# Block 4's query and key rows in spread order, and a recurrence whose decays run four groups ahead

## The reference

```python
# block 3, x: 800 rows of 256; W_aiv: 256 x 3072
a_proj, i_proj, v = jnp.split(x @ W_aiv, 3, axis=-1)
a = sigmoid(a_proj + decay_bias);  i = sigmoid(i_proj)
input_signal = jnp.sqrt(jnp.maximum(1.0 - a * a, 1e-08)) * (i * v)
h = _chunked_scan(a, input_signal)      # chunks of 64; logs clipped at 1e-10
return h @ W_mix + b_mix
# block 4, 16 heads, DK = 16
q, k, v = query @ Wq.T + bq, key @ Wk.T + bk, value @ Wv.T + bv
scores = where(mask, einsum('bhtd,bhsd->bhts', q, k) / sqrt(DK), -inf)
return softmax(scores) @ v @ Wo.T + bo
```

## Time and profile before

| | us |
|---|---|
| median of 3 runs | 506.22 |
| lowest, highest | 499.56, 510.32 |
| the profiled execution | 508.15 |
| its span | 506.4 |
| the recurrence, first projection to last of `h @ W_mix` | 233.44 to 330.54 |
| block 4's first maximum | 352.18 |
| block 4's last output projection ends | about 492 |

### The profile page before, as it was taken

One profiled execution on the slowest core, in us unless ns is written; L12 is line 12 of the kernel. 1 busy time (PEld: TensorE's weight loads), 2 busy tenths in 40 slices (PEclk: granted clock), 3 DMA queues, 4 the chain that ended last, 5 costly groups with the idle time before them and its releaser, 6 DMA issues.

```text
span 506.4 us, 7332 instructions
## 1 busy us (share of the span) xinstructions
PE 429.4 (85%) x2920; PEld 280.8 (55%) x2920; DVE 265.5 (52%) x481; ACT 163.3 (32%) x334; POOL 130.1 (26%) x174
## 2 busy tenths in 40 slices
PE   2999986959999974997999999961979969979986
PEld 1556743535667754874555557640346646646654
DVE  5056676992146520236675998651953634643423
ACT  0440430004531231322537424021143534523731
POOL 4620075327441066056100000006003213300100
PEclk9999998969999886999999999995575795975989
DMA  8991020001116963320000029976175256320002
GB/s 242 363 246 37 1 63 27 0 0 45 44 45 192 370 262 113 84 71 20 1 2 0 0 37 134 126 128 90 37 111 75 38 71 91 62 31 2 3 1 65
DMA packets 30616, 42.17 MB, mean 83 GB/s; under 512 B 4330, under 2 KB 27286, under 8 KB 30186
## 3 DMA queue, kind: packets, MB, share of 16 engines
q1 hardware_dynamic: 28279, 35.95, 28.6%
q0 software_dynamic: 2304, 5.76, 7.1%
HBM read 33.00 MB, written 8.98 MB: 83 GB/s over the span
## 4 chain that ended last, share of the span: by engine, by line
PE 65%; DVE 11%; DMA 10%; POOL 6%; ACT 4%; issue 3%; SPq 1%; ACTq 0%; DVEq 0%; POOLq 0%
PE banks L1193 13%; PE banks L1259 6%; PE banks L951 5%; PE banks L1299 5%; PE banks L1286 5%; DMA RC<-NT 4%; PE banks L1006 4%; PE banks L980 3%; PE banks L1227 3%; PE banks L940 2%; DVE RA L449 2%; PE banks L1031 2%; PE banks L1112 2%; PE banks L1130 2%; DMA RC<-q_parts 2%
## 5 line engine op out<-in xcount | busy, mean ns | idle before, releaser
L1604 DVE TENSOR_REDUCE NM<-banks 100x2 f32<-100x722 f32 x64 | 57.2, 906 | 63.2 <-PE banks L1259 62.4
L1193 PE MATMUL banks<-XT,RBG 128*128 128x400 f32 x192 | 65.0, 500 | 2.1 <-ACT XT L744 2.1
L1193 PEld LDWEIGHTS banks<-XT,RBG 128*128 128x128 f32 x192 | 36.3, 190 | 29.8 <-issue 1.2
L899 ACT ACTIVATE CT<-banks 128x400 f32<-128x400 f32 (+1 forms) x72 | 35.9, 504 | 41.9 <-PE banks L1286 40.8
L598 POOL TENSOR_TENSOR rstd<-ve,mhalf 100x4 f32<-100x4 f32 x12 | 12.5, 1040 | 140.0 <-DVE ve L1359 140.0
L744 ACT ACTIVATE XT<-banks 128x800 f32<-128x800 f32 x14 | 11.6, 838 | 98.6 <-PE banks L940 98.6
L1259 PE MATMUL banks<-RBG,RC 97*100 97x361 bf16 x64 | 23.1, 464 | 13.6 <-DMA RC<-q_parts 12.2
L940 PE MATMUL banks<-identf,XN 100*128 100x100 f32 x112 | 17.1, 309 | 17.5 <-DVE XN L1364 10.0
L1299 PE MATMUL banks<-CT,RV 128*17 128x100 f32 (+1 forms) x576 | 28.4, 293 | 0.0
L1286 PE MATMUL banks<-RC,RBG 100*128 100x100 bf16 (+1 forms) x192 | 21.7, 254 | 7.6 <-DMA RC<-NT 7.6
L1286 PEld LDWEIGHTS banks<-RC,RBG 100*128 100x128 bf16 (+1 forms) x192 | 18.3, 140 | 15.4 <-DMA RC<-NT 8.7
(11 more groups left out here) (228 smaller groups left out, 832.8 us busy)
## 6 DMA issues: line engine op xcount, KB each, us to landing
RA<-in_L_ffn_W SPq DMA_DIRECT2D x2, 2048.0 KB, 11.8
k_parts<-RA SPq DMA_DIRECT2D x18, 180.5 KB, 3.4
RBG<-in_L_attn_W_aiv SPq DMA_DIRECT2D x1, 3072.0 KB, 16.1
CT<-in_ctx_t SPq DMA_DIRECT2D x2, 1444.0 KB, 11.4
RC<-q_parts SPq DMA_DIRECT2D x12, 200.0 KB, 6.7
RBG<-k_parts SPq DMA_DIRECT2D x12, 180.5 KB, 8.8
RA<-k_parts SPq DMA_DIRECT2D x12, 180.5 KB, 9.1
RBG<-k_parts POOLq DMA_DIRECT2D x12, 180.5 KB, 6.5
```

Source lines behind the costliest of these rows:

```text
L899: sc.activation(P4[slot][0:n, g * HG * T:(g + 1) * HG * T], PS[4 + w % 2][0:n, 0:HG * T], ACT.Exp).then_inc(st_exp, 1)
L1193: ins = mm(PS[2 * aiv_pair(i) + g][:, 0:GC], WA[:, k, c:c + P], XT[:, k, GC * g:GC * g + GC], start=(k == 0), stop=(k == KT - 1))
L1604: v.tensor_reduce(NM[:, b % 2, 2 * i:2 * i + 2], PP[w % 2][0:T, :, 0:S], AX.X, ALU.max, negate=True).then_inc(mx_out, 1)
```

## The change

In the recurrence TensorE projects a0 to a3 first, then i and v of a group and the a of the group four further on. The order is a list, `AIV`, and all waits are looked up in it. The running decay is scanned into `UU[:, j]`, which is not yet in use, and capped there in an instruction of its own; the square root, floored, is multiplied with it into `SQ[j]` (`weight`), from a alone. Only then ScalarE may write the sigmoid of i into `UU[:, j]` (`weights_done`). `SQ` has eight slots. i times v, that times the weight, and the scan of the states follow (`states`). POOL writes the zero column of `UU` group by group, and block 5's weights are made behind the fourth group's states. In block 4, row r of a part's product d is now `6 * d + r` instead of `16 * r + d`, for queries and keys alike: each transfer still writes 16 partitions, every sixth one.

```diff
+AHEAD = 4
-        SQ = [part(CTF, 808 * i, B, TP) for i in range(4)]
-        CD = part(CTF, 808 * 4, B, TP)
+        SQ = [part(CTF, 808 * i, B, TP) for i in range(7)] + [part(RA, 6464, B, TP)]
-                    queue.dma_start(QS[DK * r:DK * r + DK, g].rearrange("d (k h) n -> d k (h n)", h=HK),
+                    queue.dma_start(QS[r:ROW_MASK:len(PARTS), g].rearrange("d (k h) n -> d k (h n)", h=HK),
-                queue.dma_start(KS[s][DK * r:DK * r + DK].rearrange("d (k h) s -> d k (h s)", h=HK),
+                queue.dma_start(KS[s][r:ROW_MASK:len(PARTS)].rearrange("d (k h) s -> d k (h s)", h=HK),
+        AIV = [(0, j) for j in range(AHEAD)] + [
+            x for j in range(RT) for x in [(1, j), (2, j)] + [(0, j + AHEAD)] * (j + AHEAD < RT)]
...
+            def sigmoids(w, j):
+                act.wait_ge(aiv_mm, AIV.index((w, j)) + 1)
+                if w == 1:
+                    act.wait_ge(weights_done, j + 1)
...
+            for j in range(AHEAD):
+                sigmoids(0, j)
+                if j >= 1:
+                    squares_of(j - 1)
+            squares_of(AHEAD - 1)
+            roots_of(range(AHEAD))
+            for j in range(AHEAD):
+                sigmoids(1, j)
+                sigmoids(0, j + AHEAD)
+                if j >= 1:
+                    squares_of(j + AHEAD - 1)
+            squares_of(RT - 1)
+            roots_of(range(AHEAD, RT))
+            for j in range(AHEAD, RT):
+                sigmoids(1, j)
...
+            def decays(j):
+                bt, cd = BT[j % 2], UU[:, j]
...
+                v.tensor_tensor_scan(flat(cd), flat(DEC[:, j]), flat(bt), 0.0, ALU.mult, ALU.max
+                                     ).then_inc(cdec, 1)
+                dve.wait_ge(cdec, j + 1)
+                v.tensor_scalar(flat(cd), flat(cd), 1.0, None, ALU.min).then_inc(capped, 1)
+            def weight(j):
+                dve.wait_ge(roots, j + 1)
...
+                v.scalar_tensor_tensor(out=flat(SQ[j]), in0=flat(SQ[j]), scalar=1e-4, in1=flat(UU[:, j]),
+                                       op0=ALU.max, op1=ALU.mult).then_inc(weights_done, 1)
+            def states(j):
...
+                v.tensor_tensor(o, o, src, ALU.mult).then_inc(iv_done, 1)
...
+                v.tensor_tensor(flat(UU[:, j]), flat(SQ[j]), flat(UU[:, j]), ALU.mult).then_inc(u_done, 1)
...
+            clamp(0)
+            for j in range(AHEAD):
+                if j + 1 < AHEAD:
+                    clamp(j + 1)
+                decays(j)
+            for j in range(AHEAD):
+                weight(j)
+            for j in range(AHEAD):
+                states(j)
+                clamp(j + AHEAD)
+                decays(j + AHEAD)
...
+            for j in range(AHEAD, RT):
+                weight(j)
+            for j in range(AHEAD, RT):
+                states(j)
```

More of the change, by code:

```diff
@@ L189, in build @@
         CTF = CT[:].rearrange("p k s -> p (k s)")
-        SQ = [part(CTF, 808 * i, B, TP) for i in range(4)]
-        CD = part(CTF, 808 * 4, B, TP)
-        BT = [part(CTF, 808 * (5 + i), B, TP) for i in range(2)]
+        SQ = [part(CTF, 808 * i, B, TP) for i in range(7)] + [part(RA, 6464, B, TP)]
+        BT = [part(SELT[:].rearrange("p a b -> p (a b)"), 808 * i, B, TP) for i in range(2)]
         V4 = part(RV, 0, B * NJ, H, VW)
@@ L315, in build @@
         clamped = sem("clamped")
+        capped = sem("capped")
+        weights_done = sem("weights_done")
+        u_pads = sem("u_pads")
         iv_done = sem("iv_done")
@@ L438, in k_buffer, with aiv_pair @@
             return b % 2 if b < 6 else b - 4
-        def aiv_pair(i):
-            return (i + 2) % 4
+        AIV = [(0, j) for j in range(AHEAD)] + [
+            x for j in range(RT) for x in [(1, j), (2, j)] + [(0, j + AHEAD)] * (j + AHEAD < RT)]
+        SIGS = [x for x in AIV if x[0] < 2]
+        def aiv_pair(w, j):
+            return (AIV.index((w, j)) + 2) % 4
         def y_before(L):
@@ L703, in _ @@
             gp.memset(DEC[:, :, :, 0:1], 0.0)
-            gp.memset(UU[:, :, :, 0:1], 0.0)
             for t in BT:
@@ L709, in _ @@
             bias(3)
+            for j in range(RT):
+                pool.wait_ge(weights_done, j + 1)
+                gp.memset(UU[:, j, :, 0:1], 0.0).then_inc(u_pads, 1)
             rsqrt(4)
@@ L853, in _ @@
             act.wait_ge(pads, 1)
[L854 to L865, removed]
-                act.wait_ge(clamped, j + 1)
[L867 to L875, removed]
@@ new lines, in sigmoids @@
+            def sigmoids(w, j):
+                act.wait_ge(aiv_mm, AIV.index((w, j)) + 1)
+                if w == 1:
+                    act.wait_ge(weights_done, j + 1)
+                for g in range(G):
+                    src = PS[2 * aiv_pair(w, j) + g][:, 0:GC].rearrange("p (b t) -> p b t", b=GB)
+                    if w == 0:
+                        ins = sc.activation(DEC[:, j, GB * g:GB * g + GB, 1:TP], src, ACT.Sigmoid,
+                                            bias=CB[:, C_DEC + j:C_DEC + j + 1])
+                    else:
+                        ins = sc.activation(UU[:, j, GB * g:GB * g + GB, 1:TP], src, ACT.Sigmoid)
+                ins.then_inc(sig, 1)
@@ new lines, in squares_of, with roots_of @@
+            def squares_of(j):
+                act.wait_ge(clamped, j + 1)
+                sc.activation(SQ[j], DEC[:, j], ACT.Square).then_inc(squares, 1)
+            def roots_of(js):
+                for j in js:
+                    act.wait_ge(squares, j + 1)
+                    sc.activation(SQ[j], SQ[j], ACT.Sqrt, scale=-1.0, bias=onesf[:, 0:1]).then_inc(roots, 1)
+            for j in range(AHEAD):
+                sigmoids(0, j)
+                if j >= 1:
+                    squares_of(j - 1)
@@ L1189, in aiv @@
             def aiv(i, g):
-                j, w = i // 3, i % 3
+                w, j = AIV[i]
                 for k in range(KT):
                     c = w * REC + j * P
-                    ins = mm(PS[2 * aiv_pair(i) + g][:, 0:GC], WA[:, k, c:c + P], XT[:, k, GC * g:GC * g + GC],
-                             start=(k == 0), stop=(k == KT - 1))
+                    ins = mm(PS[2 * aiv_pair(w, j) + g][:, 0:GC], WA[:, k, c:c + P],
+                             XT[:, k, GC * g:GC * g + GC], start=(k == 0), stop=(k == KT - 1))
                 return ins
@@ L1206, in _ @@
                 if i >= 4:
-                    jp, wp = (i - 4) // 3, (i - 4) % 3
+                    wp, jp = AIV[i - 4]
                     if wp < 2:
-                        pe.wait_ge(sig, 2 * jp + wp + 1)
+                        pe.wait_ge(sig, SIGS.index((wp, jp)) + 1)
                     else:
@@ L1542, in flat, with clamp @@
                 return t.rearrange("p b t -> p (b t)")
-            def inputs(j):
-                dve.wait_ge(roots, j + 1)
-                v.scalar_tensor_tensor(out=flat(UU[:, j]), in0=flat(SQ[j % 4]), scalar=1e-4, in1=flat(UU[:, j]),
-                                       op0=ALU.max, op1=ALU.mult).then_inc(u_done, 1)
+            def clamp(j):
+                a_t = DEC[:, j, :, 1:TP]
+                dve.wait_ge(sig, SIGS.index((0, j)) + 1)
+                v.tensor_scalar(a_t, a_t, FLOOR, 1.0, ALU.max, ALU.min).then_inc(clamped, 1)
+            def decays(j):
+                bt, cd = BT[j % 2], UU[:, j]
+                dve.wait_ge(clamped, j + 1)
+                v.tensor_scalar(bt[:, :, 1 + CHUNK:2 + CHUNK], DEC[:, j, :, 1 + CHUNK:2 + CHUNK],
+                                1.0 / FLOOR, None, ALU.mult).then_inc(reset64, 1)
+                dve.wait_ge(reset64, j + 1)
+                v.tensor_tensor_scan(flat(cd), flat(DEC[:, j]), flat(bt), 0.0, ALU.mult, ALU.max
[3 more added lines that the diff above has]
+            def weight(j):
+                dve.wait_ge(roots, j + 1)
+                dve.wait_ge(capped, j + 1)
+                v.scalar_tensor_tensor(out=flat(SQ[j]), in0=flat(SQ[j]), scalar=1e-4, in1=flat(UU[:, j]),
+                                       op0=ALU.max, op1=ALU.mult).then_inc(weights_done, 1)
+            def states(j):
+                dve.wait_ge(sig, SIGS.index((1, j)) + 1)
+                dve.wait_ge(aiv_mm, AIV.index((2, j)) + 1)
+                o = UU[:, j, :, 1:TP].rearrange("p (g b) t -> p g b t", g=G)
+                src = PP[aiv_pair(2, j)][:, :, 0:GC].rearrange("p g (b t) -> p g b t", b=GB)
+                v.tensor_tensor(o, o, src, ALU.mult).then_inc(iv_done, 1)
+                dve.wait_ge(iv_done, j + 1)
+                dve.wait_ge(u_pads, j + 1)
+                v.tensor_tensor(flat(UU[:, j]), flat(SQ[j]), flat(UU[:, j]), ALU.mult).then_inc(u_done, 1)
                 dve.wait_ge(u_done, j + 1)
@@ L1553, in _ @@
             dve.wait_ge(pads, 1)
[L1554 to L1585, removed]
@@ L1586, in _ @@
-            for j in range(RT - 4, RT):
-                inputs(j)
+            clamp(0)
[9 more added lines that the diff above has]
+                decays(j + AHEAD)
```

(11 more changed lines are left out.)

## The result

| | before | after |
|---|---|---|
| median, us | 506.63 (499.56 to 510.32, 4 runs) | 478.18 (477.83 to 479.65, 4 runs) |
| profiled execution, us | 508.15 | 479.65 |
| its span, us; mean granted clock | 506.4; 0.885 | 477.9; 0.929 |

The ratio is 0.9488, 95% interval 0.9389 to 0.9587: faster. The forecast was 476 us.

The account below looks back on a forecast made before the run. TensorE was taken to bound the recurrence; block 4 lost time to query loads, three row-maximum stalls and half clock behind them. 508.15 + 5.2 - 4.7 - 11.7 - 21.0 = 476 us, range 466 to 505 (0.85).

Parts of the forecast that it names:

- main case: Whole kernel: spread loads reach 260 GB/s, all three block 4 stalls and their half clock go, 476 us; chance 0.50.
- First wait: Recurrence: TensorE waits for i0's sigmoid, behind the first weight and a table load; +2.7 us.
- Middle: Recurrence: VectorE's round of 7.1 us fits within three projections of 8.1 us; no wait, 0.
- Second wait: Recurrence: i4's sigmoid comes at 294.1, TensorE wants that pair at 292.0; +2.2 us.
- rival D: Recurrence: its new gaps lower the clock; 481 to 491 us with faster loads (0.05), 518 to 528 with slow ones (0.04).
- End: Recurrence: last v's product waits 2.6 us where 1.15 stood, +1.4; the last state is no longer waited for, -1.2.
- Queries: Block 4's start: first half of the query loads takes 4.7 us at 260 GB/s instead of 9.6; -4.7 us.
- Stalls: Block 4: TensorE's three stalls for the row-maximum parts all go as key loads end sooner; -11.7 us.
- Clock: Block 4: without stalls, 52 us of half clock become 31; -21 us.
- rival B: Block 4: stalls shrink but remain; 484 to 492 us at one or two places (0.16), 502.6 if everywhere (0.10).
- C: Block 4: loads don't speed up, rows per transfer or the DRAM side counts; 513.4 us, chance 0.11.
- E: Recurrence: gains all 2.3 us, with no wait for i0; 468 us, chance 0.04.

Follow-up runs that it names:

- E1: Kernel before with only block 4's query and key rows spread to every sixth partition, recurrence as before: 474.17 us, ratio 0.9447.
- E2: Kernel after with block 4's rows turned back to 16 neighbours, so the recurrence's change alone: 505.52 us, ratio 1.0036.
- E5: Kernel before with spread rows and POOL issuing the keys of batch b + 2 ahead of its wait for batch b's maxima: 471.42 us, ratio 0.9277.
- E3: Kernel before with each query and key transfer writing every second partition, recurrence as before: 478.29 us, ratio 0.9564.
- E7: Kernel before with each query and key transfer writing every third partition, recurrence as before: 487.89 us, one run.
- E6: Kernel after with POOL issuing the keys of batch b + 2 ahead of its wait for batch b's maxima: 477.6 us, ratio 0.9412.
- E4: Kernel before, rows and recurrence unchanged, with POOL issuing the keys of batch b + 2 ahead of its wait for batch b's maxima: 488.62 us, ratio 0.9657.

## Why the prediction was right

The mechanism held: the rows alone give the gain (E1), the stalls went with the loads, and the clock rose with the stalls. The median is 2 us from the forecast, the profiled execution 3.7. That it is no more is partly luck: in the table below 4.2 us lie ahead of everything that the change touches, and the errors of the other five terms (-2.0, -0.9, +1.5, +1.6 and -0.6) cancel almost wholly. Three steps failed though the sum held: the second wait of the recurrence, the clock behind the first wait, which the main case left at full rate, and the length of a key load. The split of the 28.5 us between the two profiled executions, term by term:

| | forecast | measured |
|---|---|---|
| ahead of the second half of the recurrence | 0 | +4.2 |
| recurrence | +5.2 | +3.2 |
| end of `h @ W_mix` to the first maximum | -4.7 | -5.6 |
| block 4, stalls | -11.7 | -10.2 |
| block 4, clock and the rest | -21.0 | -19.4 |
| behind block 4 | 0 | -0.6 |
| sum | -32.2 | -28.4 |

- **Ahead of it.** The second half of the projections starts at 243.54 instead of 239.38. Of that 2.5 us stood already at 235.90 against 233.44; the other 1.7 are a fall of the clock over the first 12 matmuls (5.96 us instead of 4.27; 0.52 from 236.7 to 240.1). The change touches nothing there. The five experiments with the old recurrence start between 240.1 and 245.5, so 239.38 is the earliest of all traces; it is variation from one execution to the next. My sum had no term for it, and none could be read from one trace.
- **First wait**, forecast 2.7: 2.42. The path was the one named: weight, table load, sigmoid.
- **Middle**: no wait, as forecast.
- **Second wait**, forecast 2.2: none. Here the working failed. i4's sigmoid was ready at 297.3 (296.38 + 0.9) and wanted at 297.9 (263.69 + 12 projections of 2.70 + 1.8). TensorE came 1.8 us later than I had it, since the clock fell behind the first wait (rival D in small, priced at 1.7 for the shortest stretch), and VectorE's side came 1 us sooner. Had the clock held, a wait of some 1.2 us would have stood in its place, an estimate from these times.
- **End**, forecast +1.4 - 1.2: 1.39 where 1.15 stood is +0.2, and the last state's 1.18 is gone. The last v was projected at 308.6, about where I had it (304.9 on the scale of before, 309.1 here), but VectorE ended its three states at 309.1 already and its product at 309.96 instead of 311.7. Its first weight was ready at 294.9 where my working has 296.1 on this scale, and the weights and states behind it took a little less each than I priced them. So the sum of +3.2 is +2.4 + 1.8 + 0.2 - 1.2. All three kernels with this recurrence take 94.4 us for it.
- **Queries**, forecast 4.7: first issue to landing 7.0 us, as forecast (6.9), -4.6. But it is now held by the issue: the six take SP 3.77 us instead of 2.66, and the last lands 3.81 us after its own issue, where it took 9.34. Unforeseen is 1.0 us from the first store of a query part to the first load, 3.13 us instead of 4.17. In all six kernels with strided rows it is 3.1 to 3.3, in the three with neighbours 3.7 to 4.5. In the kernel before the first load waits for that store to land; after, it comes right behind SP's issue of the third store, at 346.40. The slow key loads of batches 2 and 3, issued from 318 on and running until about 336 in the kernel before, are in the stores' way there; that is my reading, no run tried it alone.
- **Stalls**, forecast 11.7 gone: 10.2. The load's length was mis-sized: I divided all its bytes by 260 GB/s and got 4.3 us (404.0 and 4.3 are 408.3, where the prediction has 408.5), and it takes 5.2 to 5.5 from first byte to last. The parts still land 2.3 us behind the last key byte (402.42 and 400.1), 2.5 in the prediction. With a margin of 0 that leaves about 1 us, and two short waits of 1.0 and 0.6 us remain, in batches 3 and 5. That batches 2 and 4 become cases like 3 where the clock is up is shown by E2, with waits of 1.1 and 2.1 us there.
- **Clock**, forecast 21: 45 us less of half clock by the factor 0.4 are 18. The 6.9 us left stand behind one of the short waits: rival B at one place, with a price of 2.8 us and not 8. The other 1.4 us may be in part the batches, at full clock 11.5 us apart (E5) where I had 11.8.

The rivals: C falls with E1, E3 and E7, since 16 rows per transfer, 320 packets and the same DRAM side move 1.8 times as fast at step 6 (4.5 us of engine time where 8.0 stood) and 1.4 times at step 3 (5.9) when only the partitions change. D came in its smallest form, with 3.4 us. E is refuted in every trace of the new recurrence. The change as a whole is a large gain by the rows, less what the recurrence takes. That is 3.2 us in the traces, 6.2 between the medians of E5 and E6, and 1.8, not told from nothing, in E2; the runs don't settle it closer.

## What to carry to other kernels

- When loads keep the DMA engines busy at a third of the rate that others reach in the same trace (128 GB/s and 398), look at which partitions they write before the bytes: here a changed stride gave 44% of the engine time back, with no byte and no instruction less.
- A short stall in dense work is to be priced with the clock behind it (here 17 to 20 us at 0.50 behind stalls of 3.8 to 4.1 us); and if the stall comes from two transfers that meet, moving one of them earlier is a second, independent way out. Both together were the best.
- Before running work ahead of an engine that is the bound, count what that engine waits for at the first switch: here a table load of 1.28 us behind the first weight, a wait of 2.42 us, in a stage that had only 2.3 us to give.

## What the runs showed of the hardware

- SP issued six query transfers onto strided partitions in 3.76 to 4.08 us (steps 2, 3 and 6) and onto neighbours in 2.65 to 2.80. POOL took 3.0 to 3.1 us for six key transfers in both cases.
- A wait of 2.41 to 2.42 us between dense f32 matmuls was followed by 3.4 us at 0.50 in all three kernels that had it (E2, E6, after); waits of 0.4 to 1.1 us were followed by half clock in one execution (after, 6.9 us) and not in others (E1, E2, E3, E4, E7).
- Behind stalls of about 4 us the half clock lasted 17 to 20 us in the kernel before and 10.2 in E2 (4.1 and 4.3 us), at the same work. Behind a wait of 1.4 us (E7) or 2.1 (E2) it was 6.8, behind 1.9 (E7) or 5.3 (E4) it was 10. So in these traces the length of the wait did not set it, and behind like stalls it differed between two of them by a factor of up to two.
